# The state store of a graph kernel's edge passes, issued by SyncE in place of ScalarE

## What is computed

```python
# gat (five times): h = x @ W
logit = leaky_relu((h @ a_src)[src] + (h @ a_dst)[dst], 0.2)
# dot (once)
e = leaky_relu(sum(k[src] * q[dst], -1), 0.2)
# multi (three times, 4 heads, e are the edge features)
scores = einsum('ehd,ehd->eh', q[dst], k[src]) / sqrt(16) + e @ We[i]
# all of them
p = exp(scores - segment_max(scores, dst)[dst])
agg = segment_sum(p * v[src], dst) / segment_sum(p, dst)
# multi, between two layers
emsg = gelu(concat([h[src], h[dst], e]) @ Wem[i] + bem[i])
e = layernorm(e + emsg) * ge[i] + be[i]
```

## Time and profile before

| | us |
|---|---|
| median of three runs | 11025.69 |
| lowest, highest | 11007.56, 11034.42 |
| the profiled execution | 11023.42 |
| its span, first to last instruction | 11021.6 |

### The profile page before, as it was taken

How to read it: one execution, slowest core, us unless ns; L and a number is a source line. 1 busy time by engine, 2 the same in 40 slices (tenths; PEclk the granted TensorE clock), 3 DMA queues, 4 the chain that set the end, 5 groups by cost and what they waited for, 6 DMA issues and landing times. The chain is left out here.

```text
span 11021.6 us, 85857 instructions
## 1 busy us (share of the span) xinstructions
PE 5311.2 (48%) x22037; PEld 4393.4 (40%) x22037; DVE 6580.8 (60%) x10518; ACT 4672.2 (42%) x5209; POOL 8175.1 (74%) x7864
## 2 busy tenths in 40 slices
PE   5344326885885886787688200011112433343343
PEld 5344325774774775676577200011111222232122
DVE  6333325664664665566566455445555688858887
ACT  0110005664664665565566222223333455535553
POOL 7888885776776776776777677767776777767775
PEclk8555557996996997898799555555555566656665
DMA  5333333232332232232355333324343455535553
GB/s 189 34 37 34 34 21 92 79 84 49 82 80 56 75 82 67 64 80 76 79 133 133 92 118 115 113 87 132 126 131 101 159 179 175 173 116 175 180 172 104
DMA packets 693312, 1131.50 MB, mean 103 GB/s; under 512 B 403255, under 2 KB 468070, under 8 KB 685558
## 3 DMA queue, kind: packets, MB, share of 16 engines
q0 software_dynamic: 364224, 383.74, 18.5%
q1 hardware_dynamic: 265088, 397.86, 11.1%
q10 hardware_dynamic: 63926, 349.09, 7.9%
HBM read 674.29 MB, written 468.68 MB: 104 GB/s over the span
## 5 line engine op out<-in xcount | busy, mean ns | idle before, releaser
L873 POOL DMA_INDIRECT turned<-d_t,idx x6076 | 5920.6, 974 | 1864.8 <-issue 1859.6
L1026 PE MATMUL banks<-pair,hot 128*128 128x462 f32 x13720 | 3173.9, 394 | 677.2 <-DVE wide L1121 583.3
L1026 PEld LDWEIGHTS banks<-pair,hot 128*128 128x128 f32 x13720 | 2755.8, 202 | 1094.4 <-DVE wide L1121 676.4
L647 POOL DMA_INDIRECT d_acc<-work,idx x784 | 1241.4, 1583 | 250.3 <-issue 234.7
L1183 DVE COPY idx<-src 128x28 int32 x252 | 46.7, 185 | 2173.2 <-DMA turned<-d_t,idx 2167.2
L1262 DVE TENSOR_TENSOR_SCAN wide<-banks,wide 128x224 f32<-128x224 f32 (+1 forms) x1008 | 1024.1, 1078 | 5.8
L926 ACT ACTIVATE hot<-wide,row 128x896 fp32r<-128x896 f32 x980 | 930.1, 1030 | 80.1 <-DMA wide<-d_key 49.3
L1058 PE MATMUL banks<-ident,wide 128*128 128x128 f32 x588 | 163.9, 425 | 1560.2 <-ACT wide L893 897.0
L997 ACT COPY wide<-wide 128x924 f32<-128x924 f32 (+1 forms) x252 | 476.9, 1892 | 974.6 <-DVE wide L1262 968.5
L1244 DVE TENSOR_TENSOR wide<-turned,banks 128x1792 f32<-128x1792 f32 x252 | 860.6, 3415 | 0.0
L935 ACT ACTIVATE hot<-hot 128x2688 fp32r<-128x2688 f32 (+1 forms) x280 | 773.4, 2811 | 0.3
(11 more groups left out here) (287 smaller groups left out, 8813.7 us busy)
## 6 DMA issues: line engine op xcount, KB each, us to landing
d_e<-wide ACTq DMA_DIRECT2D x168, 924.0 KB
turned<-d_t,idx POOLq DMA_INDIRECT x6076
d_e<-wide ACTq DMA_DIRECT2D x84, 1008.0 KB
wide<-d_b SPq DMA_DIRECT2D x60, 1344.0 KB
wide<-d_key SPq DMA_DIRECT2D x145, 448.0 KB, 3.7
wide<-d_b SPq DMA_DIRECT2D x60, 896.0 KB, 4.6
d_b<-wide SPq DMA_DIRECT2D x28, 1344.0 KB, 8.5
wide<-d_edge SPq DMA_DIRECT2D x84, 448.0 KB, 7.9
```

The lines of the kernel that those rows point to most:

```text
L647: gp.indirect_dma_start(g.d_acc[r][:, :], offset(idx[:, b, k:k + 1]), sums[:, b, k, :], None, compute_op=ALU.add).then_inc(added[b][r], 16)
L873: gp.indirect_dma_start(rows[:, b, k, :], None, table[:, :], offset(idx[:, b, k:k + 1])).then_inc(s["gathered"][b], 16)
L1026: mm = nc.tensor.matmul(ps_cols[i], hot[:, place, i, j, :], flat(g.pair[:, part, j]), start=(j, part) == (0, 0), stop=(j, part) == (SETS - ...
```

## The change

SP issues the store of `state`, in the iteration of the same chunk, behind the chunk's loads and ahead of the zero fill or the edge copy. It waits for the same count of `states_turned` as ACT did. ACT's wait and issue are gone; its wait for `stored` ahead of L997 remains. `sp_steps` is a count that nobody waits for.

```diff
@@ -845,6 +845,9 @@
                 sp.sem_inc(s["sp_steps"], 1)
                 sp.wait_ge(s["hot_made"], chunk + 3)
                 sp.dma_start(keys, step_keys(chunk + 4)).then_inc(s["keys_loaded"], 16)
+            sp.sem_inc(s["sp_steps"], 1)
+            sp.wait_ge(s["states_turned"], chunk + 3)
+            sp.dma_start(edge_rows(states)[:, cols, :], state[:]).then_inc(s["stored"], 16)
             if clear is not None:
                 sp.dma_start(edge_rows(clear)[:, cols, :], mid(zeros[:], K)).then_inc(s["e_stored"][b], 16)
             if kind == "dot":
@@ -997,8 +1000,6 @@
             nc.scalar.copy(state[:, :, 0:FA], values[:, b, 0:FA, :].rearrange("p f k -> p k f"))
             act.wait_ge(s["states_done"], chunk + 1)
             nc.scalar.copy(state[:, :, FA:], values[:, b, FA:, :].rearrange("p f k -> p k f")).then_inc(s["states_turned"], 1)
-            act.wait_ge(s["states_turned"], chunk + 3)
-            act.dma_start(edge_rows(states)[:, cols, :], state[:]).then_inc(s["stored"], 16)
 
         pairs(act, one)
         act.wait_ge(s["tails_shifted"], 1)
```

## The result

| us | before | after |
|---|---|---|
| median | 11030.06 (11007.56 to 11038.13, 4 runs) | 11114.52 (11112.48 to 11117.1, 4 runs) |
| profiled execution, its span | 11023.42, 11021.6 | 11117.1, 11115.3 |

The account below looks back on a forecast made before the run. POOL's issue of gathers was taken to bound the kernel; 54 us in the update passes, 8 at pass ends and 0 from ACT gave 62 us more, 11088 us on the median's footing, range 11022 to 11155.

Parts of the forecast that it names:

- The bound: All passes: POOL's issue of gathers sets the pace, 37.07 us per chunk in the update passes.
- the update term: Update passes: edge rows queued behind the store lengthen the loop to 38.1 us, over POOL's 37.1; 54 us in two passes.
- T: Time from the store's issue to the landing of the edge rows; taken as 6.3 us, bounds 4.3 and 8.3.
- The wait at L1191: Update passes: DVE would wait there for the edge rows, some 3 us per chunk, where it waited for ACT 1.7.
- Rival 1: Update passes: edge rows come soon enough, T at most 5.3 us, POOL keeps the pace; 11026 to 11034 us; chance 0.25.
- Rival 2: Update passes: the store is slow, T near 8.3 us, loop 40.1 us, 156 us lost, time 11190; chance 0.12.
- Rival 3: All passes: ACT is the hidden bound and gives back 126 us, time 10900; chance 0.03 together with any other gain.
- Keys, b rows, e_m rows at 0: SP's loads: keys' issue unmoved, b rows some 5 us later but in time, e_m rows land before needed; 0 us.
- Multi 0 at 0: Multi pass without update: edge rows land later, but `we_rows` come 6 us before DVE needs them; 0 us.
- The end of the clear pass: Last chunk: the zero fill behind the store lands 11.8 us after the store's issue, before 5.1; +6.7 us, once.
- Behind the dot pass: Last chunk of the dot pass: the 448 KB edge copy behind the store adds 1.2 us, once.
- Inside the clear pass: Zero fill issued after the store has a whole chunk's time to land within the pass; 0 us.

Follow-up runs that it names:

- e1b: Against the kernel before, SP issues the store in the two update passes only, ACT in the others; 11066.62 us, ratio 1.0046 to the kernel before.
- e9: Against the changed kernel, the multi passes issue the next chunk's edge rows behind the same wait but ahead of the store; 11042.69 us, ratio 1.0029 to before.
- e8: Against the changed kernel, SP issues the edge rows behind the b rows too, both behind the store; 11345.45 us, ratio 1.0302 to the kernel before.
- e6: Against the changed kernel, edge rows, zero fill and edge copy all stand ahead of SP's wait, only the store behind it; 11017.58 us, ratio 1.0000 to before.
- e7: Against the kernel before, store left on ACT, but the clear pass's zero fill waits for its chunk's state; 11044.86 us, ratio 1.0026.
- e5b: Against the changed kernel, the clear pass's zero fill is issued ahead of SP's new wait; 11075.79 us, ratio 1.0053 to the kernel before.
- e3: Against the changed kernel, only the next chunk's edge rows are issued ahead of SP's wait; 13663.21 us in a 13.8 ms session, ratio 0.9868 to before.
- e11: Against the changed kernel, edge rows, fill and copy ahead of SP's wait, fill in 1536 B pieces; 13603.6 us in a 13.8 ms session, ratio 0.9857 to before.

## Why the prediction was right, and where it was not

- **The bound and the update term.** Forecast: T 6.3 us, loop 38.1, 54 us in both passes (unrounded, its own terms give 38.08-37.07 = 1.01 us per chunk, 53 us). Measured: T 0.61 to 0.98 plus 5.7, 6.3 to 6.7 us; 38.24 us per chunk (L1192 from 8725.24 to 9719.55, 26 steps); 54.8 us by L1192's first and last starts in both passes. That the last number meets the forecast so closely is in part luck: over the 26 steps per pass that the forecast counts it is 58.8, and the first step of each pass, 39.9 and 40.7 us before, gives 4.0 back. e1b shows the term alone (+51), e9 shows it undone by T of 3.9, and in e8 T of 11.2 made it five times as large (292 us in the update passes and behind them, against 55.9). The choice between the bounds, to liken the store to the b rows and not to the zero fill, was the one that the runs bear out.
- **The wait at L1191, "some 3 us per chunk".** It is 5.6. The sentence forgot that DVE already waited there for ACT, 2.16 us in a tight chunk: the edge rows' delay comes on top, 2.2+3.6 = 5.8. The loop was computed from starts, so the sum wasn't touched.
- **The rival "nothing moves" and the rule for it.** Rival 1 was priced by T below 5.3 and a time of 11026 to 11034. It is wrong for this kernel, and e9 shows that it is right for another order: there T is 3.9 and the update passes move by -3 us. Of the Trainium skill's page "DMA: Bandwidth & Descriptors" the prediction named two sections. With "Queues, rings and completion order", by which a ring is worked off in order, the traces agree (3.9, 6.3 to 6.7, 11.2 us for three orders), though no run tells the ring from the 16 shared DMA engines. With "Issuing engines are not separate DMA queues", by which another issuer saves only its sequencer's time, e6 agrees (ratio 1.0000); it was wrong to conclude from it that the sum could be 0, since it says nothing of what the moved DMA and its wait delay behind them.
- **Rival 2, the slow store.** T would have been 8.3; it is 6.3 to 6.7. **Rival 3, ACT's 126 us.** None of it is in e6.
- **Keys, b rows, e_m rows at 0.** No pass shows a longer wait for the keys or the b rows: ACT waits 48.8 us in all for the keys (before 49.3) and 39.9 for the b rows (before 39.8), and nothing waits for the e_m rows. In the update passes SP's b rows land after 9.8 us, long before their use.
- **Multi 0 at 0.** In the chunk looked at, the first copy of the turns starts 7.3 us behind the store's issue (8030.58 to 8037.85) in place of 2.5, 4.7 us later, against the forecast's "some 5 us later with the same pace", and DVE still waits for the gather in 24 chunks. The pass and what follows took 5.0 us more; the same pass of other kernels here lies between 971 and 990 us, so I don't read these 5 us as the change.
- **The end of the clear pass.** Forecast +6.7, measured +6.8. Timeline of SP at the end of the clear pass of after, store, last fill, first load of the next layer:

```profile
6133.08 0.33 SPq L850 DMA_DIRECT2D d_e<-wide  x1
6133.45 0.44 SPq L852 DMA_DIRECT2D d_b<-wide  x1
6144.79 0.34 SPq L1383 DMA_DIRECT2D w_sb<-in_l_w  x1
```

  11.7 us from the store to the next layer, 11.8 forecast, 5.1 before. Behind the dot pass 1.2 were forecast. From its last store to the next layer it takes 6.8 us (7316.67 to 7323.50), 5.1 before (7287.15 to 7292.27): +1.7. The whole stretch is 3.3 longer, but 1.2 and 2.0 longer in e1b and e7 too, in which SP stores nothing in the dot pass, so the rest isn't told from the scatter.
- **Inside the clear pass: the step that failed.** "Within the pass they have a whole chunk's time", the reason for putting the late fill at 0 there, asked only when the fill must have landed, which is late enough. It didn't ask what the fill takes from others while it runs. The gathers on which the pace of that pass rests run at the same time, and with the fill 8 us later in the chunk their rows come later: +18.6 us, shown by e7 and e5b. A row of before could have raised the question: SP's issue right behind a fill took over 5 us.
- **The sum.** +93.7 by spans against 62: of the 31.7 us in between, 18.6 are the clear pass, 2 each the update passes with what follows them and the dot pass's end, and the other 9 lie in passes where nothing can be told from the scatter. The time lies in the span that the forecast gave for a T of 5.9 to 7.2 (11064 to 11132), but not by T alone: without the term put at 0 it would be 19 us lower.

## What to carry to other kernels

When a DMA that waits for a late result is moved to another engine's list, look at what that list issues next, for whom, and how soon it is needed: here 84.5 us were lost to what four kinds of issue (store, edge rows, zero fill, edge copy) had ahead of them, and all of them came back (ratio 1.0000) when the edge rows and the two writes stood ahead of the wait. If a load has to stay behind the same wait, issue it ahead of the large store, not behind it. And of a transfer that nobody waits for, ask not only when it lands but what runs beside it.

## What the runs showed of the hardware

- One load of 448 KB landed 3.9 us after its issue with nothing large right ahead (e9), 5.7 with a store of 1008 KB ahead in the same engine's queue (after), 9.6 with 1344 KB of loads besides (e8). The last step is 0.34 us per 100 KB, more than the 0.27 read from multi 0. Whether the same store in another queue would delay it as much is not shown.
- A zero fill of 1344 KB in pieces of 384 B that was issued 8 us later in the chunk held up another engine's gathers (after, e7): 4.5 us of POOL's pause in place of 1.0, four times in the pass, and SP's own next issue took 6.6 us in place of 5.3.
- The same kernel took 11.0 ms in two sessions and 13.8 ms in two others, with DVE, ACT and POOL busy within 1% of the same time and PE 2 to 4% more. Idle time moved: DVE's waits for gathered rows fell from 2167 us to some 700, and about 2000 us came up at the line that adds PE's products. There two kernels with SP as the issuer and the edge rows ahead of the wait (e3, e11) were 1.3 to 1.4% faster than the kernel before, where at 11.0 ms such a kernel (e6) was the same.
